# Moving eight dense units ahead of the first sum, and the weight loads behind the first node rows, in three graph layers

## The reference

```
def _mean_aggregate(x, src, dst, n):
    summed = segment_sum(x[src], dst, n)
    deg    = segment_sum(ones, dst, n)
    return summed / maximum(deg, 1)[:, None]
def _sage_conv(x, src, dst, Wl, bl, Wr, n):
    return _mean_aggregate(x, src, dst, n) @ Wl.T + bl + x @ Wr.T
x = layernorm(x + relation_layer(x, ...))           # layer 0
h = relu(sage_conv(x, src, dst, W1l, b1l, W1r))      # layer 1
h = relu(sage_conv(h, src, dst, W2l, b2l, W2r))      # layer 2
out = layernorm(x + sage_conv(h, src, dst, W2l, b2l, W2r))   # layer 3
```

## Time and profile before

| what | us |
|---|---|
| median of three runs | 3321.13 (3313.59 to 3326.47) |
| the profiled execution, its own time | 3326.72 |
| its span, first to last instruction | 3323.2 |
| layer 0 ends, layer 1 begins | about 1555 |
| layer 2, layer 3 begin | about 2139, 2719 |

### The profile page before, as it was taken

One profiled execution on the slowest core, in us unless ns is written; L12 is line 12 of the kernel. 1 busy time (PEld: TensorE's weight loads), 2 busy tenths in 40 slices (PEclk: granted clock), 3 DMA queues, 4 the chain that ended last, 5 costly groups with the idle time before them and its releaser, 6 DMA issues. The chain is left out here.

```text
span 3323.2 us, 53365 instructions
## 1 busy us (share of the span) xinstructions
PE 2852.0 (86%) x16283; PEld 2436.2 (73%) x16283; DVE 2414.4 (73%) x5400; ACT 2130.6 (64%) x3761; POOL 2416.0 (73%) x2281
## 2 busy tenths in 40 slices
PE   5569999989899999995899999588999958899995
PEld 4458888877788778874778788477878847778784
DVE  7968888888888888885566666456666645777776
ACT  1067777777777777772677777267777726677771
POOL 5267777777777777774777777577777757777773
PEclk7579999999999999997999999789999979999997
DMA  4256656666666656665666665466666546666663
GB/s 135 75 145 169 168 157 170 167 166 166 165 167 167 163 156 167 167 165 165 198 191 189 192 191 179 150 218 188 192 190 189 180 154 208 196 198 198 206 193 91
DMA packets 327859, 572.41 MB, mean 172 GB/s; under 512 B 47877, under 2 KB 225878, under 8 KB 327574
## 3 DMA queue, kind: packets, MB, share of 16 engines
q0 software_dynamic: 105696, 290.56, 32.1%
q1 hardware_dynamic: 218361, 275.92, 26.2%
q10 hardware_dynamic: 3517, 2.48, 0.3%
HBM read 494.21 MB, written 74.56 MB: 171 GB/s over the span
## 5 line engine op out<-in xcount | busy, mean ns | idle before, releaser
L1475 POOL DMA_INDIRECT rows_arena<-table_h,src_idx x1224 | 1304.7, 1066 | 460.4 <-issue 369.9
L1475 POOL DMA_INDIRECT rows_arena<-table_scaled_x,src_idx x782 | 830.1, 1062 | 280.1 <-issue 273.6
L2038 PE MATMUL bank<-wide_counts,h_pairs 128*128 128x512 f32 x3528 | 876.1, 400 | 0.0
L2038 PEld LDWEIGHTS bank<-wide_counts,h_pairs 128*128 128x128 f32 x3528 | 661.5, 193 | 137.5 <-DVE h_pairs L1820 0.7
L1975 PE MATMUL bank<-rel_pairs,ftype_hot 125*128 125x258 f32 x4688 | 711.7, 299 | 53.5 <-ACT ftype_hot L1601 50.7
L1812 DVE TENSOR_TENSOR row_pairs<-rows_arena,row_pairs 128x1024 fp32r<-128x1024 f32 x306 | 373.5, 1221 | 450.2 <-ACT row_pairs L1610 448.5
L1975 PEld LDWEIGHTS bank<-rel_pairs,ftype_hot 125*128 125x128 f32 x4688 | 622.4, 192 | 88.6 <-ACT ftype_hot L1601 50.8
L1610 ACT CAST row_pairs<-rows_arena 128x1024 fp32r<-128x1024 f32 x306 | 320.1, 1046 | 476.5 <-DMA rows_arena<-table_h,src_idx 468.0
L1998 PE MATMUL bank<-row_pairs,rel_pairs 128*128 128x256 f32 x2448 | 392.5, 306 | 182.3 <-DVE row_pairs L1812 182.1
L1622 ACT CAST wide_counts<-rows_arena 128x1024 fp32r<-128x1024 bf16 (+1 forms) x450 | 501.9, 1115 | 0.0
L1998 PEld LDWEIGHTS bank<-row_pairs,rel_pairs 128*128 128x128 f32 x2448 | 339.3, 203 | 214.3 <-issue 209.1
(11 more groups left out here) (186 smaller groups left out, 3106.5 us busy)
## 6 DMA issues: line engine op xcount, KB each, us to landing
rows_arena<-edge_counts SPq DMA_DIRECT2D x234, 512.0 KB, 4.0
edge_counts<-fcount SPq DMA_DIRECT2D x48, 832.0 KB, 6.3
rows_arena<-in_edge_type_dram SPq DMA_DIRECT2D x195, 187.5 KB
rows_arena<-table_h,src_idx POOLq DMA_INDIRECT x1224, 3.6
rows_arena<-table_h SPq DMA_DIRECT2D x36, 512.0 KB, 12.1
rows_arena<-table_scaled_x,src_idx POOLq DMA_INDIRECT x782
table_h<-chunk_info SPq DMA_DIRECT2D x96, 128.0 KB, 4.2
rows_arena<-in_x_dram SPq DMA_DIRECT2D x6, 1024.0 KB
```

What stands on the lines that cost most here:

```text
L1475: pool.indirect_dma_start(out=rows[:, g % ring, c, :], out_offset=None, in_=table[:, :], in_offset=bass.IndirectOffsetOnAxis(ap=src_idx[:, ...
L2038: last = pe.matmul(bank[2 + h][:, 0:PASS_COLS], h_pairs[:, v % HALVES, part, b % HALF, h * P:(h + 1) * P], wide_counts[:, v % HALVES, b % ...
```

## The change

`BEFORE = 8` units get slot -1: PE runs them ahead of its slot loop, so ahead of `sums(0)`. The other 286 units are spread from slot 1 on to the same last slot, 91, which makes it three, three and four units a slot. The halves follow: halves 0 to 3 stand ahead of `row_highs(0)` on ScalarE and ahead of the first `window_hots` and of `row_lows(0)` on VectorE. Halves 4 and 5 (tile 2) stand in slot 0, halves 6 and 7 (tile 3) in slot 1, half 8 (tile 4) in slot 2. SP now issues batch 0, tiles 0 and 1, batch 1, the two weights (256 KB each), batches 2 to 12, and then, still in slot 0, tiles 2, 3 and 4. The start slots of some node blocks move by one or two; the last four blocks of layers 1 and 2 keep theirs (102, 105, 106, 107), and layer 3 has 121 slots where it had 122.

```
+BEFORE = 8
-unit_slot = [3 + u * (groups - 3 - EARLY - (WD - 1)) // units + u // NB for u in range(units)]
+unit_slot = [-1 if u < BEFORE else
+             1 + (u - BEFORE) * (groups - 1 - EARLY - (WD - 1)) // (units - BEFORE) + u // NB
+             for u in range(units)]
-half_slot = [max(0, min(unit_slot[u] for u in range(units) if half_of(u) == v) - 1)
              for v in range(0 if first else WD * HPW)]
+half_slot = [max(-1, min(unit_slot[u] for u in range(units) if half_of(u) == v) - 1)
              for v in range(0 if first else WD * HPW)]
 # SP
-if not first:
-    sp.dma_start(w_l[:, :, :], weights[Wl][:, :, :]).then_inc(s_weights, 16)
-    sp.dma_start(w_r[:, :, :], weights[Wr][:, :, :]).then_inc(s_weights, 16)
 sp.wait_ge(s_start, 1)
...
     load_batch(0)
     for t in range(ATILES):
         load_tile(t)
-    for i in range(1, len(s_h)):
+    load_batch(1)
+    sp.dma_start(w_l[:, :, :], weights[Wl][:, :, :]).then_inc(s_weights, 16)
+    sp.dma_start(w_r[:, :, :], weights[Wr][:, :, :]).then_inc(s_weights, 16)
+    for i in range(2, len(s_h)):
         load_batch(i)
 for t in range(ATILES, WD * TPW):
-    if max(half_slot[v] for v in range(len(half_slot)) if tile_of_half(v) == t - ATILES) == s:
+    if max(0, max(half_slot[v] for v in range(len(half_slot)) if tile_of_half(v) == t - ATILES)) == s:
         load_tile(t)
 # ScalarE, slot 0
+for v in halves_at(-1):
+    half_highs(v)
 row_highs(0)
 # VectorE, ahead of the slots
+for v in halves_at(-1):
+    half_lows(v)
 for g in range(min(HOTS - 1, groups)):
     window_hots(g)
 row_lows(0)
 # PE, ahead of the slots
+for u in range(units):
+    if unit_slot[u] < 0:
+        dense_unit(u)
```

More of the change, by code:

```diff
@@ L1322, in half_blocks @@
                 return b, min(HALF, NB - b)
-            half_slot = [max(0, min(unit_slot[u] for u in range(units) if half_of(u) == v) - 1) for v in range(0 if first else WD * HPW)]
+            half_slot = [max(-1, min(unit_slot[u] for u in range(units) if half_of(u) == v) - 1) for v in range(0 if first else WD * HPW)]
             def halves_at(slot):
```

## The result

The changed kernel is slower: 3353.08 us (3351.72 to 3355.90, four runs) against 3323.80 (3313.59 to 3333.24, four runs). The ratio is 1.0088 [1.0062, 1.0115], about 29 us. The profiled execution took 3353.56 us, its span was 3349.6 where it was 3323.2, and its granted TensorE clock was 0.929 of full speed.

A forecast was written before the change was run, and what follows sets the result against it. GpSimd's unbroken gathers were taken as the bound. Waits at the 25th gather of 5.3 + 8.2 + 8.2 = 21.7 us, other terms about nothing, made about +21 on 3321: 3342 us, range 3316 to 3356.

The forecast's parts named there:

- The sum: All terms over layers 1 to 3: about +21 us, all as idle time of GpSimd, from 3321 to 3342 us.
- What bounds the kernel: Layers 1 to 3: GpSimd issues gathers without a stop, about 1.37 us each; PE, ScalarE and VectorE follow it.
- the hold: GpSimd's wait for `row_lows(2)` at its 25th gather, handed on from ScalarE's wait for tile 2; loss 21.7 us.
- The first four halves: Start of a layer, before GpSimd's 17th gather: they just fit, value nothing, at worst 1 or 2 us a layer.
- The chain: Slot 0: ScalarE waits for tile 2, delaying `row_highs(2)`, `row_lows(2)` and the 25th gather; 5.2 us from cast to `row_lows`.
- When tile 2 lands: SP's queue, behind all batches and weights: tile 2 is there 35.4 us into layer 1, 35.9 into layers 2 and 3.
- the piece: The 106 KB load ahead of tile 2 in SP's queue, reckoned by its bytes: +0.4 us.
- The weights' +1.5: 512 KB of weights ahead of batches 2 to 12 in SP's queue: net +1.5 us, bounds 0 and 2.1.
- the third rival: Gathers' own length changes as VectorE's work shifts: 14 us over three layers, either way; no separate chance given.
- After it: Behind the 25th gather: `row_lows(3)` fits by half a microsecond, at worst 1 to 2 us a layer; nothing regains lost time.
- Tile 2 in time: First rival, SP's loads: tile 2 lands early enough or gathers are not held; no change, 3321 us; chance 0.14.
- PE as the bound: Second rival: eight units come off PE's path, 7.7 us a layer, 23 us, giving 3298 us; chance 0.03.

The follow-up runs named there:

- the change again: The changed kernel itself, unaltered, run on another chip, against the kernel before on that chip: 3356.32 us, ratio 1.0096 [1.0072, 1.0120].
- the tiles-between kernel: Changed kernel with only SP's load order altered, tiles 2 to 6 each issued ahead of a batch: 3321.29 us, 0.9989 against the kernel before.
- the piece last: Changed kernel with only batch 12 (106 rows, 106 KB) issued behind tiles 2 and 3: 3342.57 us, ratio 1.0049 against the kernel before.
- the weights alone: Kernel before with only the weights moved behind batch 1, on the slower chip: 3926.36 us, ratio 1.0019 against the kernel before there.

## Why the prediction was right, and where its sizes were off

The sum gave 3342 us and slower, with the range 3316 to 3356. The time was 3353.08: slower, in the range, 11 us above the sum. Measured as a difference it is 29 us where the sum said 21.

- **What bounds the kernel.** Right on this chip. Taking the hold away gave the loss back (0.9989 [0.9972, 1.0007]), PE's eight units gave nothing that can be told from that, and gathers longer by 64 us made the span longer by 70.
- **The first four halves fit.** Right. The first `half_highs` started 5.3 us into the layer, PE's first units at 1562.6, and GpSimd's 17th gather wasn't held.
- **The chain.** Right in each link: tile 2, ScalarE's cast of counts, `row_highs(2)`, `row_lows(2)`, the 25th gather, once a layer. The steps behind the landing were given 5.2 us and took 5.2, with GpSimd's pause of 0.3 us on top.
- **When tile 2 lands.** This is the step that was mis-sized: "I take +3.7 (bounds 1.9 and 4.6): tile 2 is there 35.4 us into layer 1". It was there at 38.2, 38.7 and 38.6 us into the layers (in layer 2 by the start of ScalarE's cast), past even the upper bounds of 36.3 in layer 1 and 36.8 in layer 3. The larger part is the piece and the tile: they were given 0.4 + 1.8 us and took 3.5, 4.3 and 4.9. Without the piece the tile took 1.9 to 2.1, so the piece, reckoned by its bytes, is the term that failed. The weights' +1.5 was +3.0 in layer 1 (batch 11 from 31.7 to 34.7), +2.0 in layer 2 and +1.5 in layer 3, and 1.8 to 2.1 in the change again. At the front batch 0 landed 5.3 us behind the first gather of layer 1 where it was 5.7, but tile 1, two loads on, at 8.9 as before. Putting the weights first again gave only 1.0 us a layer, and batch 11 still came 0.9 to 1.7 us later than before the change; that part isn't the weights' and stays unassigned.
- **The sum.** 21.7 us of loss at the three starts were 30.7. From there on 3.4 us came back, inside the 14 us that the third rival gave to the gathers' length. The tail of layer 3 gave 1.6 where at most 1 was said, and that of layer 2 took as much.
- **After it.** Right: the four other waits of GpSimd for `row_lows` in layer 1 are 1.2 us together, and `row_lows(3)` fitted: it ended 4.4 us behind `row_lows(2)`, 0.8 us before GpSimd wanted it, where half a microsecond was reckoned.
- **Idle time of ScalarE.** Forecast some 10 us in front of half 4, measured 20.8: it came to that cast at 1571.8 already. It changes nothing in the sum, since only its end counts.
- **The rivals.** Tile 2 in time: it fell, since `row_lows(2)` ended 43.4 to 43.8 us into the layers and not by 32.9. It is what the tiles-between kernel makes true, and the price, no change, was met there. PE as the bound: fell on this chip; its condition holds on the slower one. The gathers' own length: present as a few microseconds, and not to be steered by VectorE's selection matrices.

The prediction also weighed the rule (the Trainium skill, DMA: Bandwidth & Descriptors, Queues, rings and completion order) by which the rested gathers would leave the tile all the engines and take 2 us off the sum. The runs don't show that for tile 2. GpSimd issued its 24th gather 31 us into layer 3 of the changed kernel, but that gather's rows landed only at 37.6, 1 us before tile 2, so the two shared the engines nearly to the end; with the piece last they landed together in layer 1 (1590.6 and 1590.7). Tile 3 then landed 1.2 to 1.3 us behind tile 2 in layers 1 and 3 of both traces, less than the 2.1 us between loads beside gathers. That agrees with the rule, though loads overlap and such a distance isn't quite a rate.

The best version is the change with the tiles between the batches: 3321.29 us, level with before (0.9989 [0.9972, 1.0007]), and 0.9948 [0.9925, 0.9972] on the slower chip. A ring of five quads, which would let GpSimd run on over part of the hold, wasn't tried, and neither was a last batch cut so that it uses more engines.

## What to carry to other kernels

When work is moved ahead, move the loads that it needs ahead as well, in the one queue that issues them: list that queue in order, and put beside each load the time at which it is first read. An instruction that waits for a late load on an in-order engine holds everything queued behind it, so look for what feeds the bounding engine there; here ScalarE had time to spare, and its stand of 20.8 us still cost GpSimd 8 to 11 us a layer. Look at the shape of each load in that list and not at its bytes alone: one of 106 rows took some 2.4 us of the queue. And ask first whether the engine that gains is the one that bounds: eight units off PE were worth nothing where GpSimd sets the pace.

## What was not expected of the hardware

- One program took 3324 us on one chip and 3922 on another, at a granted clock of about 0.927 and 0.874. A trace of the slower chip (the weights alone) has pauses of up to 13.7 us on ScalarE that nothing of the core ends. Experiments on a kernel must each have the kernel before on the same chip.
- A load of 106 rows and 106 KB in a full queue put off the 512 KB load behind it by about 2.4 us, more than five times what its bytes take. Just ahead of the late landing the busy share of the 16 DMA engines was 0.14, about two of them.
- A gather can be lengthened when a VectorE instruction with two inputs in SBUF is running as it starts, to 0.2 us past the end of that instruction or the next (1.95 us in place of 0.95); many that start so aren't. Leaving out `window_hots`, which ends most of these waits, didn't shorten the gathers on the mean (1062 and 1075 ns against 1067 and 1066), and one with a single SBUF input in its place made them 1119 ns.
